# Attention and feed-forward layer on one core: the filler placed behind the values, small sums of the group normalisation on ScalarE, and three planned DMA times

## The chip, the cores and the metric

The kernel runs on one core of a Trainium2 chip. The metric is the device time of one execution in microseconds, the median of several runs. Engines are named as the profile names them: PE is TensorE's matmul, PEld its weight load, DVE is VectorE, ACT is ScalarE, POOL is GpSimd, SP is SyncE.

## The reference

The input x has the shape (4, 1024, 512). The layer is a differential attention, a group normalisation, an output projection, a residual and a layer normalisation, and behind them a feed-forward network with ternary weights, a residual and a layer normalisation.

```
q, k, v = x @ Wq, x @ Wk, x @ Wv          # 16 heads, 4 key/value heads, rotary positions
s1, s2  = q1 @ k1.T * scale + causal, q2 @ k2.T * scale + causal
diff    = softmax(s1) - lam * softmax(s2)
out     = diff @ v                        # (B, H, T, 64)
mean, var over (T, 64) of each head       # the group normalisation
out     = ((out - mean) * rsqrt(var + 1e-5) * gn_w + gn_b) * (1 - LAMBDA_INIT)
x       = layernorm(x + out @ Wo)
x       = layernorm(x + (silu(x @ up) * (x @ gate)) @ down)   # ternary weights
```

## The kernel before, in words

**Attention.** The work is 512 units of one query tile (128 rows) of one head, in both maps. Each goes through a chain over the engines: `scores` on PE (L1077, q against k, up to 1024 keys, one or two matmuls a map), `minimum` on DVE (L1421, mask, negative maximum, PSUM to SBUF), `exponent` on ACT (L1215), `factor` on POOL (L1346, L1347), `combine` on DVE (L1492, the difference of the two maps), `turn` on PE (L1058 and L1062, transposes of 128x128 blocks), `evict` on ACT (L1205, PSUM to SBUF), `values` on PE (L1096, a product with v that writes 64 of the 128 PSUM rows at a time, 32 or 48 matmuls in a run), and `product` on DVE (L1513, divides by the sums of the exponentials and writes `ra`). Long and short tiles alternate, so that four units always make the same amount of work. There are 129 runs of `values`.

**Group normalisation.** After eight pairs of units (a chunk; there are 32) DVE takes the statistics of `ra` (`moments`, L1518 to L1520), PE averages the mean over 64 rows with a tiny matmul (`mean`, L1181), DVE computes `spread`, four operations on one column each (L1526 to L1529: mean minus averaged mean, a copy of the averaged mean out of PSUM, the square, plus the variance), PE averages that (`variance`, L1184), DVE adds epsilon (`deviation`, L1533), POOL makes the factors and applies them (`group`, L1389 to L1392; `settle`, L1395), and SP stores the chunk (`store a`). A chunk's first `product` waits for the store of the chunk two before it, whose half of `ra` it writes.

**Filler.** Between the steps of the attention chain PE runs `fill` pieces: the projections of all batches (L1120, L1127, float32 weights loaded by ACT's queue into two buffers, `load w`, and x into six homes, `load x`), and, as soon as a batch's attention is stored, the output projection (L1141), the transposes of x1 (L1145), the up and gate products (L1154) and the down product (L1163). A piece takes about 1.7 us. In the first batch there is only projection to fill with.

**Who orders it.** The order on every engine is fixed when the kernel is built, by a list scheduler in the file (`in_order`, L495). It has a table of costs (`takes`), a table of what comes before what (`after`), the times at which DMAs count as landed behind their issue (`LANDS`), and strings of steps for each engine (`STRINGS`); it steps through planned time and gives each engine one head at a time. On PE it takes, of the heads that could start within a small window behind the earliest, the one of the lowest rank: scores (rank 0, window 0.4 us), mean, variance and totals (1), turn (2, 0.25 us), values (3), filler last and only if it is the earliest (4, 0.0). From unit 128 on scores are held to 3.75 us a unit. PSUM has eight banks; scores may hold four. The planned times set only the order: on the chip the engines wait for semaphores, and the instruction streams of each engine run strictly in the planned order.

The choice on PE, L616 and L617:

```
soon = min(h[0] for h in heads)
return min((h for h in heads if h[0] <= soon + FIRST[h[2].what][1]), key=lambda h: (FIRST[h[2].what][0], h[0]))
```

Of the kernel before, what the change touches and what calls it, by code (L numbers as in the profile page):

```python
# [10 lines left out]
ACT = mybir.ActivationFunctionType  # L11
ALU = mybir.AluOpType
# [24 lines left out]
CHUNKS = NH // 16  # L37
# [102 lines left out]
OF_KIND = {_kind: [j for j in PROJECTION + MIXING if j.kind == _kind] for _kind in PIECES}  # L140
# [59 lines left out]
def y_last(b):  # L200
# [6 lines left out]
TERN_AT = [100 + int(3 * i) for i in range(PREP)]  # L207

HAND_OVER = {"pe": .3, "act": .4, "dve": .3, "pool": .3}
LANDS = {"load q": 4.5, "load k": 7.5, "load v": 6.0, "store v": 7.0, "store rotated": 6.0, "store a": 4.5, "load a": 6.5,  # L210
         "store out": 2.5, "load wo": 9.0, "load x1": 8.0, "load weight": 12.0, "load x": 6.5, "load w": 6.5, "load rope": 5.0, "load lambda": 6.0, "load first": 2.5}


def width(n):
# [16 lines left out]
def takes(item):  # L231

    what, a, b = item
    if what == "scores":
        return 0.00042 * width(a) + (0.04 if width(a) > BANK else 0.03)
    if what == "turn":
        return 0.109 * blocks_of(a, b)[0] + 0.02
    if what == "values":
        return sum(0.22 * (STEPS[heads_of(duo)[0]].t + 1) for duo in duos_of(a)) + 0.24
    if what == "fill":  # L240
        return COST[a.kind] + 0.02
    if what == "exponent":
        return 0.27 + 0.00084 * width(a)
    if what == "evict":
        blocks, keys = blocks_of(a, b)
        if in_line(STEPS[a].duo) or blocks == keys:
            return 0.06 + 0.107 * blocks
        return 0.22 + (0.06 + 0.107 * keys if keys else 0)
    if what == "minimum":
        return 0.08 + 0.00104 * width(a)  # L250
    if what == "combine":
        return 0.13 + 0.00104 * width(a)
    if what == "empty":
        return {"E": 1.25, "O": 1.25, "wo": 1.5, "x1T": 0.61, "up": 0.61, "gate": 0.61,
                "y": 1.55 if a.i else 0.67}[a.kind]
    if what == "factor":
        return 1.4 if STEPS[a].r else 1.15
    return {"mean": 0.2, "variance": 0.2, "totals": 0.2, "copy": 0.55, "hidden": 0.55, "sum": 1.1,
            "lambda": 0.3, "normalise": 0.65, "high": 0.63, "early": 3.1, "product": 0.22, "moments": 1.55,
            "spread": 0.5, "deviation": 0.16, "ternary": 1.25, "all sums": 0.3, "scales": 0.3, "constants": 0.7, "minus lambda": 0.2,  # L260
            "load q": 1.0, "load k": 1.9, "load first": 0.5, "load x1": 0.5, "load wo": 0.48, "load a": 0.5, "store v": 0.45,
            "store rotated": 0.45, "store a": 0.45, "store out": 0.5, "load weight": 0.5, "load v": 0.5, "load lambda": 0.8, "lambda sums": 0.5,
            "hidden low": 1.32, "rsqrt": 1.5, "rotate": 1.35, "low": 1.3, "group": 1.5, "settle": 1.25, "side": 1.1}.get(what, 0.06)


def after(item):

    what, a, b = item
    out = []
# [96 lines left out]
        if a % 8 == 0 and a >= 16:  # L366
            out.append(ITEM("store a", a // 8 - 2))
    elif what == "moments":
        out = [ITEM("product", 8 * a + 7)]
    elif what == "spread":  # L370
        out = [ITEM("mean", a)] + [ITEM("settle", a - 1)] * (a > 0)
    elif what == "deviation":
# [65 lines left out]
def stored(b, h, u):  # L438
# [10 lines left out]
           [ITEM(what, c) for c in range(CHUNKS) for what in ("mean", "variance")], [ITEM("totals")]],  # L449
    "act": [[ITEM("exponent", n, m) for n, m in _maps], [ITEM("evict", n, h) for n, h in _halves],  # L450
            [ITEM("load rope", h) for h in range(2)], [ITEM("load lambda")], [ITEM("lambda")],
            *[[ITEM("copy", j) for j in OF_KIND[kind]] for kind in ("V", "x1T", "up")],
            [ITEM("hidden", j) for j in OF_KIND["gate"]], [ITEM("normalise", j) for j in LN_JOBS], [ITEM("sum", i) for i in range(PREP)],
            [ITEM("side", i) for i in range(PREP)],
            [ITEM("load x", p, c) for p in range(ONCE, len(PASSES)) for c in range(DC)], [ITEM("load w", i) for i in range(len(WLOADS))]],
# [2 lines left out]
            *[[ITEM("empty", j) for j in PROJECTION + MIXING if j.kind in kinds]  # L458
              for kinds in ("EO", ("x1T",), ("up", "gate"), ("wo", "y"))],
            [ITEM("early", j) for j in O_JOBS[:ROT_FIRST]], [ITEM("high", j) for j in O_JOBS[ROT_FIRST:]],  # L460
            [ITEM(what, c) for c in range(CHUNKS) for what in ("moments", "spread", "deviation")],
            [ITEM("lambda sums"), ITEM("minus lambda")], [ITEM("all sums"), ITEM("scales"), ITEM("constants")],
            [ITEM("ternary", i) for i in range(PREP)]],
    "pool": [[ITEM("factor", n) for n in _heads], [ITEM("hidden low", j) for j in OF_KIND["gate"]],
# [30 lines left out]
def in_order():  # L495
# [89 lines left out]
    def choose(e):  # L585
        now = free[e]
        heads = []
        for s, string in enumerate(STRINGS[e]):
            if at[e][s] < len(string):
                item = string[at[e][s]]  # L590
                r = ready(item, e)
                if r is None:
                    continue
                if item.what == "scores" and item.a and item.b == 0:
                    if item.a >= 128:
                        r = max(r, end[ITEM("scores", item.a - 16)] + PACE * 16)
                if item.what in LONG and factors:
                    other = ITEM("combine", factors - 1)
                    if other not in end:
                        continue  # L600
                    r = max(r, end[other])
                if banks_of(item):
                    found = banks(banks_of(item))
                    if found is None or item.what == "turn" and stuck(item) and sum(map(stuck, turned)) >= STUCK:
                        continue
                    if item.what == "scores" and in_scores + len(found) > SCORE_BANKS:
                        continue
                    r = max([r] + [bank_free[m] for m in found])
                heads.append((max(r, now), r, item, s))
        if e == "pe":  # L610
            filling = next_fill(now)
            if filling:
                heads.append((max(filling[0], now), filling[0], filling[1], None))
            if not heads:
                return None
            soon = min(h[0] for h in heads)  # L616
            return min((h for h in heads if h[0] <= soon + FIRST[h[2].what][1]), key=lambda h: (FIRST[h[2].what][0], h[0]))  # L617
        if not heads:
            return None
        soon = min(h[0] for h in heads)  # L620
        return min((h for h in heads if h[0] <= soon + 0.02), key=lambda h: h[1] - AHEAD.get(h[2].what, 0.0))
# [55 lines left out]
def layer_kernel(nc, x, x_cols, w_proj, wo, lams_in, gn, w_up, w_gate, w_down, rope, out):  # L677
# [13 lines left out]
    with ctx:  # L691
# [3 lines left out]
        def sem(name):  # L695
            return ctx.enter_context(nc.semaphore(name))
# [140 lines left out]
        s_gmv = sem("s_gmv")  # L837
        s_gm = sem("s_gm")
        s_rv = sem("s_rv")
        s_gv = sem("s_gv")  # L840
        s_norm = sem("s_norm")

# [17 lines left out]
        def multiplied(eng, duo):  # L860

            if duo % 2 and duo < DUOS - 1:
                eng.wait_ge(s_short, duo // 2 + 1)
            else:
                read_out(eng, "values", run_of(duo))
# [324 lines left out]
        def _(act):  # L1190
# [36 lines left out]
            def load_w(i):  # L1227
                if i >= 2:
                    act.wait_ge(s_ffull, INDEX[W_LAST[i - 2]] + 1)
                act.dma_start(wr[:, i % 2, :, :], w_proj[UNITS.index(WLOADS[i][3])]).then_inc(s_win[i % 2], 16)  # L1230
# [23 lines left out]
            def hidden_high(job):  # L1254
                f = HID[job]
                freed(act, job)
                nc.scalar.activation(hid[:, 0, job.i % 8, :], th[:, f % NTH, :], ACT.Copy).then_inc(s_hhi, 1)  # L1257

            for what, a, b in ORDER["act"]:
                if what == "exponent":  # L1260
                    exponent(a, b)
# [13 lines left out]
                    load_x(a, b)  # L1275
                elif what == "load w":
                    load_w(a)
                elif what == "load rope":
                    half = slice(a * BANK, (a + 1) * BANK)
                    act.dma_start(cs[:, :, half], rope[:, :, half]).then_inc(s_cs[a], 16)  # L1280
# [117 lines left out]
        def _(dve):  # L1398
            chain = [0]

            def link(ins):

                chain[0] += 1
                ins.then_inc(s_link, 1)
                dve.wait_ge(s_link, chain[0])
# [80 lines left out]
            for what, a, b in ORDER["dve"]:  # L1486
# [28 lines left out]
                elif what == "moments":  # L1515
                    for duo in range(8 * a, 8 * a + 8):
                        multiplied(dve, duo)
                    nc.vector.bn_stats(gst[:, 0, :], ra[:, a % 2, 0:BANK])  # L1518
                    link(nc.vector.bn_stats(gst[:, 1, :], ra[:, a % 2, BANK:T]))
                    nc.vector.bn_aggr(gmv[:, :], gst[:, :, :].rearrange("p h s -> p (h s)")).then_inc(s_gmv, 1)  # L1520
                elif what == "spread":
                    dve.wait_ge(s_gm, a + 1)
                    if a:
                        dve.wait_ge(s_norm, a)
                    bank, _ = BANK_OF[ITEM("mean", a)]
                    link(nc.vector.tensor_tensor(gsm[:, 1:2], gmv[:, 0:1], F[bank][:, 0:1], ALU.subtract))  # L1526
                    nc.vector.tensor_copy(gsm[:, 0:1], F[bank][:, 0:1]).then_inc(s_ffree[bank], 1)
                    link(nc.vector.tensor_tensor(gsm[:, 1:2], gsm[:, 1:2], gsm[:, 1:2], ALU.mult))
                    nc.vector.tensor_tensor(gsm[:, 2:3], gsm[:, 1:2], gmv[:, 1:2], ALU.add).then_inc(s_rv, 1)  # L1529
                elif what == "deviation":  # L1530
                    dve.wait_ge(s_gv, a + 1)
                    bank, _ = BANK_OF[ITEM("variance", a)]
# [69 lines left out]
```

## Time and profile before

| | us |
|---|---|
| median of 3 runs | 2219.04 (2218.55 to 2219.58) |
| the profiled execution | 2216.09 |
| its span, first to last instruction | 2214.3 |
| PE busy | 2141.2 (97%) |
| DVE busy | 1702.5 (77%) |
| ACT busy | 1431.8 (65%) |
| POOL busy | 1187.0 (54%) |

The profile is of one execution. Its busy time on PE contains weight loads that could not be hidden and the pipeline's latency at the end of each group of matmuls, so 97% is not 97% of the peak. The attention chain runs from about 53 us to 1941 us; what remains behind it is filler alone. In a timeline's row, the start and the duration of a merged group of matmuls give its end; the distance from the end of one group to the end of the next is what the second costs.

### The profile page before, as it was taken

The numbers are of one execution on the slowest core, as the hardware profiler recorded it, in microseconds if no ns is written. First come the engines' busy times: TensorE is split into PE (matmuls) and PEld (weight loads), VectorE is DVE, ScalarE is ACT, GpSimd is POOL, SyncE is SP. The second block draws the span as 40 slices with busy tenths as digits, with TensorE's granted clock in tenths as the row PEclk, the third lists the DMA queues.
The fourth block names the chain that finished last, engine by engine and source line by source line (L and its number), as shares of the span: only waits on it lengthen the run. The fifth ranks groups of instructions, "written<-read, shape, count | busy, mean of one in ns | idle before, by whom it ended". The sixth has DMA issues, their size and how long they took to land.

```text
span 2214.3 us, 41402 instructions
## 1 busy us (share of the span) xinstructions
PE 2141.2 (97%) x13442; PEld 1380.0 (62%) x13442; DVE 1702.5 (77%) x3829; ACT 1431.8 (65%) x3322; POOL 1187.0 (54%) x1919
## 2 busy tenths in 40 slices
PE   8999999899999999999999999999999999999998
PEld 4666667566666666666766666666666666644443
DVE  4888887889889888888778888878888888733333
ACT  0667777677687777767667767767677777622232
POOL 0676666677665555555545555655554555431232
PEclk9999999999999999999999999999999999999999
DMA  7666665867761213223632323342432112021000
GB/s 263 198 213 186 200 189 186 262 187 213 219 176 61 70 49 106 82 69 114 186 92 70 93 63 89 99 129 65 142 96 77 53 49 84 24 71 53 1 20 20
DMA packets 257428, 255.49 MB, mean 115 GB/s; under 512 B 31296, under 2 KB 199360, under 8 KB 255168
## 3 DMA queue, kind: packets, MB, share of 16 engines
q1 hardware_dynamic: 246016, 220.26, 33.2%
q10 hardware_dynamic: 11200, 32.58, 4.6%
q8 instruction: 112, 1.84, 0.3%
q14 instruction: 100, 0.82, 0.1%
HBM read 181.48 MB, written 71.30 MB: 114 GB/s over the span
## 4 chain that ended last, share of the span: by engine, by line
PE 79%; DVE 8%; issue 4%; POOL 4%; ACT 3%; DMA 1%; ACTq 0%; DVEq 0%; SPq 0%; POOLq 0%
PE PS L1154 19%; PE PS L1077 10%; PE PS L1096 10%; PE PS L1141 10%; PE PS L1163 9%; PE PS L1058 9%; PE PS L1120 8%; DVE e_long L1421 2%; PE PS L1127 2%; POOL linv L1346 1%; DVE e_long L1492 1%; ACT dt_long L1205 1%; PE PS L1062 1%; ACT e_long L1215 1%; POOL coef L1347 1%
## 5 line engine op out<-in xcount | busy, mean ns | idle before, releaser
L1215 ACT ACTIVATE e_long<-e_long,nmax 128x768 f32<-128x768 f32 (+3 forms) x512 | 505.9, 989 | 207.2 <-DVE nmax L1421 201.2
L1346 POOL TENSOR_TENSOR linv<-lsum,powers 128x2 f32<-128x2 f32 x512 | 405.4, 792 | 420.4 <-ACT e_long L1215 336.5
L1421 DVE CUSTOM_DVE_ANT_0 e_long<-PS,mask_b 128x768 f32<-128x768 f32 (+3 forms) x512 | 517.3, 1020 | 73.6 <-PE PS L1077 56.1
L1077 PE MATMUL PS<-kstk,qstk 128*128 128x384 f32 (+5 forms) x1536 | 465.7, 410 | 23.3 <-DVE nmax L1421 10.9
L1077 PEld LDWEIGHTS PS<-kstk,qstk 128*128 128x128 f32 x1536 | 268.6, 190 | 157.3 <-issue 92.7
L1492 DVE SCALAR_TENSOR_TENSOR e_long<-e_long,coef 128x1024 f32<-128x1024 f32 (+3 forms) x256 | 276.9, 1082 | 67.0 <-POOL coef L1347 66.6
L1205 ACT ACTIVATE dt_long<-PS 128x512 f32<-128x512 f32 (+3 forms) x544 | 258.5, 514 | 103.9 <-PE PS L1058 99.3
L1215 ACT ACTIVATE e_short<-e_short,nmax 128x384 f32<-128x384 f32 (+3 forms) x512 | 283.8, 559 | 17.1 <-DVE nmax L1421 16.1
L1359 POOL TENSOR_TENSOR hid<-th,hid 128x512 f16<-128x512 f32 x128 | 148.0, 1159 | 255.4 <-ACT hid L1257 132.8
L1120 PE MATMUL PS<-xT,wr 128*128 128x512 f32 x560 | 267.7, 606 | 13.8 <-DMA wr<-in_w_proj 8.7
L1058 PE MATMUL PS<-ident,e_long 128*128 128x128 f32 x1664 | 239.7, 275 | 11.9 <-DVE e_long L1492 8.7
L1347 POOL TENSOR_SCALAR coef<-lsum,linv,neglam 128x1 f32<-128x1 f32 x512 | 218.3, 426 | 53.4
L1421 DVE CUSTOM_DVE_ANT_0 e_short<-PS,mask_b 128x384 f32<-128x384 f32 (+3 forms) x512 | 237.7, 486 | 10.7 <-PE PS L1062 4.6
L1163 PE MATMUL PS<-down_t,hid 128*128 128x512 fp8e4 x1024 | 234.8, 379 | 0.4 <-ACT dt_long L1205 0.3
L1058 PEld LDWEIGHTS PS<-ident,e_long 128*128 128x128 f32 x1664 | 196.6, 142 | 55.5 <-issue 17.6
L1205 ACT ACTIVATE dt_short<-PS 128x512 f32<-128x512 f32 (+3 forms) x256 | 121.2, 474 | 136.8 <-PE PS L1062 106.8
L1096 PE MATMUL PS<-dt_long,vkv 128*64 128x128 f32 x3328 | 206.2, 274 | 0.0
L1154 PE MATMUL PS<-x_hi,gate_t 128*128 128x512 f16 x512 | 194.3, 380 | 1.0 <-DVE nmax L1421 1.0
L1154 PE MATMUL PS<-x_hi,up_t 128*128 128x512 f16 x512 | 194.2, 379 | 0.3 <-ACT dt_long L1205 0.3
L1154 PE MATMUL PS<-x_lo,gate_t 128*128 128x512 f16 x512 | 194.0, 379 | 0.0
L1154 PE MATMUL PS<-x_lo,up_t 128*128 128x512 f16 x512 | 194.0, 379 | 0.0
L1096 PEld LDWEIGHTS PS<-dt_long,vkv 128*64 128x64 f32 x3328 | 188.9, 138 | 0.3 <-issue 0.3
(125 smaller groups left out, 3275.2 us busy)
## 6 DMA issues: line engine op xcount, KB each, us to landing
qstk<-dq SPq DMA_DIRECT2D x512, 128.0 KB, 2.9
dq<-hl SPq DMA_DIRECT2D x25, 1024.0 KB, 5.5
wr<-in_w_proj ACTq DMA_DIRECT2D x48, 512.0 KB, 4.5
kstk<-dk SPq DMA_DIRECT2D x64, 256.0 KB, 5.2
da<-ra SPq DMA_DIRECT2D x32, 512.0 KB, 3.3
at_sb<-da SPq DMA_DIRECT2D x32, 512.0 KB, 4.1
wt<-in_w_up SPq DMA_DIRECT2D x16, 512.0 KB, 5.7
wt<-in_w_gate SPq DMA_DIRECT2D x16, 512.0 KB, 6.1
```

The source lines that it names most:

```text
L1058: last = nc.tensor.transpose(F[bank][:, k * P:(k + 1) * P], e1_of(n)[:, col:col + P], ident[:, :])
L1077: last = nc.tensor.matmul(slot[:, h, :], qstk[:, duo % 4, 2 * r + m, :].bitcast(F32R), kstk[:, g % 2, m, h * w:(h + 1) * w].bitcast(F32R), ...
L1096: last = nc.tensor.matmul(bank[64 * r:64 * r + 64, at:at + P], vkv[:, duo // 16 % 2, kb, :], dt_of(n)[:, kb, :], start=kb == 0, stop=kb == t)
L1120: last = nc.tensor.matmul(bank[:, :], wr[:, job.i % 2, c, at:at + P], x_part(job, c), start=c == 0, stop=c == DC - 1)
L1154: last = nc.tensor.matmul(bank[:, :], w[:, c, job.i * P:(job.i + 1) * P], part[:, c, job.h * BANK:(job.h + 1) * BANK], start=c == 0 and pa ...
L1163: last = nc.tensor.matmul(bank[:, :], hid[:, part, e, job.j * P:(job.j + 1) * P], down_t[:, 8 * job.i + e, :], start=e == 0 and part == 0, ...
L1205: copied = nc.scalar.activation(dt_of(n)[:, 4 * half:4 * half + here, :].rearrange("p k q -> p (k q)"), F[bank][:, 0:here * P], ACT.Copy)
L1215: nc.scalar.activation(e, e, ACT.Exp, bias=nmax[:, u % 8:u % 8 + 1], scale=-1.0, accum_out=lsum[:, n % 4, m:m + 1]).then_inc(s_exp, 1)
L1346: link(nc.gpsimd.tensor_tensor(linv[:, a % 8, :], lsum[:, a % 4, :], mone, ALU.pow))
L1347: nc.gpsimd.tensor_scalar(coef[:, a % 2:a % 2 + 1], lsum[:, a % 4, 0:1], linv[:, a % 8, 1:2], neglam[:, :], ALU.mult, ALU.mult).then_inc(s ...
L1421: nc.vector.tensor_tensor_reduce(out, slot, mask, -1.0, -NEG, ALU.add, ALU.min, nmax[:, u % 8:u % 8 + 1]).then_inc(s_negmax, 1)
L1492: nc.vector.scalar_tensor_tensor(e1_of(a)[:, 0:w], e2_of(a)[:, 0:w], coef[:, a % 2:a % 2 + 1], e1_of(a)[:, 0:w], ALU.mult, ALU.add).then_i ...
```

## The change

Four edits in one. The planner counts three kinds of DMA as landed later: `store rotated` 8 instead of 6 us, `load x` and `load w` 8 instead of 6.5 us. On PE, when the last step given out was `values`, a `scores` head ranks behind every other head that lies in its window. `spread` moves from DVE to ACT as a string of its own, is written as four activations, and is planned with 0.9 instead of 0.5 us. And `moments` of a chunk waits until the `spread` of the chunk before has been done, because the two now run on different engines and share `gmv`. The number of x homes stays six.

```
-LANDS = {... "store rotated": 6.0, ... "load x": 6.5, "load w": 6.5, ...}
+LANDS = {... "store rotated": 8, ... "load x": 8, "load w": 8, ...}

-            "spread": 0.5,
+            "spread": 0.9,

     elif what == "moments":
-        out = [ITEM("product", 8 * a + 7)]
+        out = [ITEM("product", 8 * a + 7)] + [ITEM("spread", a - 1)] * (a > 0)

+            back = order[e][-1].what == "values" if order[e] else False
+            return min((h for h in heads if h[0] <= soon + FIRST[h[2].what][1]),
+                       key=lambda h: (back and h[2].what == "scores", FIRST[h[2].what][0], h[0]))

 # ScalarE's stream (link: the engine waits for the instruction's own semaphore)
+                elif what == "spread":
+                    act.wait_ge(s_gm, a + 1)
+                    if a:
+                        act.wait_ge(s_norm, a)
+                    bank, _ = BANK_OF[ITEM("mean", a)]
+                    link(nc.scalar.activation(gsm[:, 3:4], F[bank][:, 0:1], ACT.Copy, scale=-1.0))
+                    nc.scalar.activation(gsm[:, 0:1], F[bank][:, 0:1], ACT.Copy).then_inc(s_ffree[bank], 1)
+                    link(nc.scalar.activation(gsm[:, 1:2], gmv[:, 0:1], ACT.Square, bias=gsm[:, 3:4]))
+                    nc.scalar.activation(gsm[:, 2:3], gsm[:, 1:2], ACT.Identity, bias=gmv[:, 1:2]).then_inc(s_rv, 1)

 # VectorE's stream, moments
+                    if a:
+                        dve.wait_ge(s_rv, a)
 # VectorE's stream, spread: taken out
-                    link(nc.vector.tensor_tensor(gsm[:, 1:2], gmv[:, 0:1], F[bank][:, 0:1], ALU.subtract))
-                    nc.vector.tensor_copy(gsm[:, 0:1], F[bank][:, 0:1]).then_inc(s_ffree[bank], 1)
-                    link(nc.vector.tensor_tensor(gsm[:, 1:2], gsm[:, 1:2], gsm[:, 1:2], ALU.mult))
-                    nc.vector.tensor_tensor(gsm[:, 2:3], gsm[:, 1:2], gmv[:, 1:2], ALU.add).then_inc(s_rv, 1)
```

## Rows read from the trace of the kernel before

**Rows 1.** The page: span, and the chain that ended last by engine.

```profile
span 2214.3 us, 41402 instructions
...
PE 79%; DVE 8%; issue 4%; POOL 4%; ACT 3%; DMA 1%; ACTq 0%; DVEq 0%; SPq 0%; POOLq 0%
```

**Rows 2.** Windows by stage: busy of PE, PEld, DVE, ACT, POOL, PEclk, DMA, GB/s.

```profile
0.00:600.00 600.00, 556.54 (x3290) 376.88 (x3292) 492.62 (x1083) 388.12 (x922) 372.68 (x537) 0.98 0.69 211
600.00:1941.00 1341.00, 1320.44 (x9047) 882.67 (x9044) 1111.92 (x2590) 970.16 (x2294) 744.57 (x1277) 1.00 0.30 89
```

**Rows 3.** Waits of PE, 0 to 600 us: total us, times, longest.

```profile
PE PS L1077 <- ACT dt_long L1205: 10.1, 12, 2.8
...
PE PS L1077 <- DVE nmax L1421: 8.6, 19, 1.7
PE PS L1120 <- DVE ra L1513: 3.3, 1, 3.3
```

**Rows 4.** Waits of PE, 600 to 1941 us, the largest.

```profile
PE PS L1058 <- DVE e_long L1492: 6.7, 7, 2.3
```

**Rows 5.** Timeline of PE (start us, us): first and last scores right behind values.

```profile
88.38 0.56 PE L1077 MATMUL PS<-kstk,qstk 128*128 128x320 f32 x2
...
1912.29 0.56 PE L1077 MATMUL PS<-kstk,qstk 128*128 128x320 f32 x2
```

**Rows 6.** Timeline of PE: scores behind filler, scores behind values, turns behind scores.

```profile
916.56 0.38 PE L1154 MATMUL PS<-x_lo,gate_t 128*128 128x512 f16 x1
916.59 0.82 PE L1077 MATMUL PS<-kstk,qstk 128*128 128x512 f32 x2
...
923.04 1.48 PE L1096 MATMUL PS<-dt_long,vkv 128*64 128x128 f32 x24
924.45 0.73 PE L1077 MATMUL PS<-kstk,qstk 128*128 128x512 f32 x2
925.02 0.49 PE L1058 MATMUL PS<-ident,e_short 128*128 128x128 f32 x3
```

**Rows 7.** Timeline of PE: turns of three blocks behind values.

```profile
1383.73 0.39 PE L1096 MATMUL PS<-dt_long,vkv 128*64 128x128 f32 x4
1384.05 0.44 PE L1058 MATMUL PS<-ident,e_short 128*128 128x128 f32 x2
1384.32 0.27 PE L1062 MATMUL PS<-ident,wide 128*128 128x128 f32 x1
```

**Rows 8.** Groups by form, weight loads: xcount | busy us, mean ns of one | idle before.

```profile
L1077 PEld LDWEIGHTS PS<-kstk,qstk 128*128 128x128 f32 x1536 | 268.6, 190 | 157.3 <-issue 92.7 <-DVE nmax L1421 25.5 <-ACT dt_long L1205 6.7
...
L1058 PEld LDWEIGHTS PS<-ident,e_long 128*128 128x128 f32 x1664 | 196.6, 142 | 55.5 <-issue 17.6 <-DVE e_long L1492 14.8 <-DVE nmax L1421 4.5
...
L1163 PEld LDWEIGHTS PS<-down_t,hid 128*128 128x128 f16 x1024 | 97.8, 98 | 107.6 <-issue 3.0 <-POOL hid L1359 1.4 <-ACT dt_long L1205 0.5
```

**Rows 9.** Groups by form: one of the four small operations of spread on DVE.

```profile
L1527 DVE COPY gsm<-PS 128x1 f32<-128x1 f32 x32 | 5.1, 158 | 1.1
```

**Rows 10.** Groups by form: ACT, exponent of the narrowest tile.

```profile
L1215 ACT ACTIVATE e_short<-e_short,nmax 128x128 f32<-128x128 f32 x128 | 50.5, 399 | 4.1 <-DVE nmax L1421 4.1
```

**Rows 11.** Line 1295 on ACT: duration ns min/median/max, first and last start.

```profile
L1295 ACT ACT_TABLE_LOAD  x1: 1283/1283/1283, 5.2 to 5.2; - x1
L1295 ACT ACTIVATE th<-th x1: 203/203/203, 16.4 to 16.4; 128x2 f32<-128x2 f32 x1
```

**Rows 12.** DMA issues, 0 to 600 us: count, KB each, median us from issue to landing.

```profile
wr<-in_w_proj ACTq DMA_DIRECT2D x41, 512.0 KB, 4.5
...
dq<-hl SPq DMA_DIRECT2D x17, 1024.0 KB, 5.5
```

**Rows 13.** DMA issues, 408 to 421 us.

```profile
da<-ra SPq DMA_DIRECT2D x1, 512.0 KB, 9.3
```

**Rows 14.** Timeline of DVE around the longest wait.

```profile
419.73 0.29 DVE L1513 TENSOR_TENSOR ra<-PS,dt_long 128x128 f32<-128x128 f32 x1 [3.98 <-DMA da<-ra]
```

**Rows 15.** Window at the lower clock: length, busy PE, PEld, DVE, ACT, POOL, PEclk, DMA.

```profile
419.40:426.20 6.80, 6.12 (x10) 3.26 (x11) 6.10 (x13) 1.03 (x2) 1.52 (x2) 0.50 0.51 110
```

More of the change, by code:

```diff
@@ L209 @@
 HAND_OVER = {"pe": .3, "act": .4, "dve": .3, "pool": .3}
-LANDS = {"load q": 4.5, "load k": 7.5, "load v": 6.0, "store v": 7.0, "store rotated": 6.0, "store a": 4.5, "load a": 6.5,
-         "store out": 2.5, "load wo": 9.0, "load x1": 8.0, "load weight": 12.0, "load x": 6.5, "load w": 6.5, "load rope": 5.0, "load lambda": 6.0, "load first": 2.5}
+LANDS = {"load q": 4.5, "load k": 7.5, "load v": 6.0, "store v": 7.0, "store rotated": 8, "store a": 4.5, "load a": 6.5,
+         "store out": 2.5, "load wo": 9.0, "load x1": 8.0, "load weight": 12.0, "load x": 8, "load w": 8, "load rope": 5.0, "load lambda": 6.0, "load first": 2.5}
 def width(n):
@@ L259, in takes @@
             "lambda": 0.3, "normalise": 0.65, "high": 0.63, "early": 3.1, "product": 0.22, "moments": 1.55,
-            "spread": 0.5, "deviation": 0.16, "ternary": 1.25, "all sums": 0.3, "scales": 0.3, "constants": 0.7, "minus lambda": 0.2,
+            "spread": 0.9, "deviation": 0.16, "ternary": 1.25, "all sums": 0.3, "scales": 0.3, "constants": 0.7, "minus lambda": 0.2,
             "load q": 1.0, "load k": 1.9, "load first": 0.5, "load x1": 0.5, "load wo": 0.48, "load a": 0.5, "store v": 0.45,
@@ L451 @@
             [ITEM("load rope", h) for h in range(2)], [ITEM("load lambda")], [ITEM("lambda")],
-            *[[ITEM("copy", j) for j in OF_KIND[kind]] for kind in ("V", "x1T", "up")],
+            *[[ITEM("copy", j) for j in OF_KIND[kind]] for kind in ("V", "x1T", "up")], [ITEM("spread", c) for c in range(CHUNKS)],
             [ITEM("hidden", j) for j in OF_KIND["gate"]], [ITEM("normalise", j) for j in LN_JOBS], [ITEM("sum", i) for i in range(PREP)],
@@ L460 @@
             [ITEM("early", j) for j in O_JOBS[:ROT_FIRST]], [ITEM("high", j) for j in O_JOBS[ROT_FIRST:]],
-            [ITEM(what, c) for c in range(CHUNKS) for what in ("moments", "spread", "deviation")],
+            [ITEM(what, c) for c in range(CHUNKS) for what in ("moments", "deviation")],
             [ITEM("lambda sums"), ITEM("minus lambda")], [ITEM("all sums"), ITEM("scales"), ITEM("constants")],
@@ L616, in choose @@
             soon = min(h[0] for h in heads)
-            return min((h for h in heads if h[0] <= soon + FIRST[h[2].what][1]), key=lambda h: (FIRST[h[2].what][0], h[0]))
+            back = order[e][-1].what == "values" if order[e] else False
+            return min((h for h in heads if h[0] <= soon + FIRST[h[2].what][1]),
+                       key=lambda h: (back and h[2].what == "scores", FIRST[h[2].what][0], h[0]))
         if not heads:
@@ L839, in layer_kernel @@
         s_rv = sem("s_rv")
+        s_alink = sem("s_alink")
         s_gv = sem("s_gv")
@@ L1257, in hidden_high, with link @@
                 nc.scalar.activation(hid[:, 0, job.i % 8, :], th[:, f % NTH, :], ACT.Copy).then_inc(s_hhi, 1)
+            done = [0]
+            def link(ins):
+                done[0] += 1
+                ins.then_inc(s_alink, 1)
+                act.wait_ge(s_alink, done[0])
             for what, a, b in ORDER["act"]:
@@ L1520, in _ @@
                     nc.vector.bn_aggr(gmv[:, :], gst[:, :, :].rearrange("p h s -> p (h s)")).then_inc(s_gmv, 1)
[L1521 to L1525, printed above, removed]
-                    link(nc.vector.tensor_tensor(gsm[:, 1:2], gmv[:, 0:1], F[bank][:, 0:1], ALU.subtract))
-                    nc.vector.tensor_copy(gsm[:, 0:1], F[bank][:, 0:1]).then_inc(s_ffree[bank], 1)
-                    link(nc.vector.tensor_tensor(gsm[:, 1:2], gsm[:, 1:2], gsm[:, 1:2], ALU.mult))
-                    nc.vector.tensor_tensor(gsm[:, 2:3], gsm[:, 1:2], gmv[:, 1:2], ALU.add).then_inc(s_rv, 1)
                 elif what == "deviation":
```

## The prediction

> **What bounds the kernel now.** I read the page first, then windows by stage, the waits of PE, and its timeline group by group. PE carries 79% of the chain that ended last, and no other engine more than 8% [rows 1]: a microsecond counts if PE's work gets shorter or an idle gap of PE closes. The windows part the run in two [rows 2]. From 600 to 1941 us PE is busy for 1320.44 of 1341 us, so only 20.6 us of idle time are there to be won. From 0 to 600 us it is busy for 556.54, idle for 43.5, of which 8.65 is the start. In that stage PE waits for ACT's evictions (10.1 us at scores) nearly as much as for DVE's minima (8.6) [rows 3]; later DVE's combine is the largest (6.7) [rows 4]. Behind 1941 us there is only filler, in an order that the change doesn't touch.
>
> The busy time itself holds a part that the order decides, seen in the timeline from end to end. Scores of two 512-column matmuls behind filler: 916.94 to 917.41, 0.47 us. The same behind values: 924.52 to 925.18, 0.66 us [rows 6]. The 0.19 us more is one weight load of scores (190 ns) [rows 8], hidden elsewhere and bare behind values. Three blocks of turns behind scores cost 0.33 us (925.18 to 925.51) [rows 6], behind values 0.47 (1384.12 to 1384.59) [rows 7]: 0.14 more, again its own weight load (142 ns) [rows 8]. So the run of values hides nobody's first weights, and who follows it pays for his: 0.19 for scores, 0.14 for turns, 0.19 for a projection or output-projection piece by the same float32 kind of load, 0.10 for an up, gate or down piece (98 ns) [rows 8].
>
> **The change part by part.** *No scores behind values.* Of 129 runs of values, I count 76 with scores right behind, the first and last at 88.38 and 1912.29 us [rows 5], and 51 with turns. The exits cost 76 x 0.19 = 14.4 us now. They don't vanish: another takes the place. In 71 of the 76 places turns come right behind the one to four scores, so in most the turn was nearly ready; I take 50 of 76 going to turns (0.05 us won each, 2.5 us) and 26 to filler. The next filler behind the 76 is 35 times of the float32 kind (nothing won), 39 times up, gate or down (0.09 won), two times the transposes of x1: half of 26 x 0.09 is 1.2 us. Sum 3.7 us won. Bounds: nothing (all float32 pieces) and 76 x 0.09 = 6.8 us. The scores are late by a group of turns or by one piece of 1.7 us, and what waits for them is DVE's minimum; from 600 us on the pace rule has them early enough, and ahead of that see the rival below.
>
> The Trainium skill has a rule that speaks against this part: in TensorEngine Tiling (Array Packing), Key Properties, a change of tiling mode drains the engine, and values are tiles of 64 columns between full ones. By that the exit is paid whatever follows, and were it one fixed price the part would win nothing. The trace agrees that everyone pays and shows prices that differ by follower (0.19 against 0.14 us).
>
> *Spread to ACT.* DVE loses four operations of 0.158 us [rows 9], 0.63 us a chunk, 32 x 0.63 = 20 us of its 1702. ACT gets four. The trace has no one-column activation out of PSUM; from below it is bounded by the 128x2 activation of 203 ns [rows 11], from above by the narrowest exponent, 399 ns for 128 columns with a bias read per row [rows 10]. Four make 0.81 to 1.6 us; I take 1.0, nearer the row without columns, with two waits of ACT for itself: 32 us on top of 1432. Behind it in ACT's stream stand exponents and evictions, and for the evictions PE waits. Were PE's waits proportional to the load of who ends them, DVE's 1.2% less would give back some 0.3 us of its 20 to 30, ACT's 2.2% more would take 0.4 of its 15: nothing. Uncovered in the first 600 us, where PE is exposed, ten chunks could give 6 us (DVE) or cost 10 us (ACT). Value: 0. One sentence on a page: ScalarE: Activation LUTs, What ACT_TABLE_LOAD costs, gives 186 ns plus 93 ns for a bias per row, by which the four would be some 0.93 us, an estimate; no run here shows it yet.
>
> *moments waits for the spread before.* That was done a chunk (about 60 us) earlier: nothing. The chain of a chunk gets some 0.5 us longer, and its store is needed only when the second chunk behind begins.
>
> *Loads counted as later.* Nothing on the chip takes another time; only the plan changes. In the first 600 us `load w` lands in a median 4.5 us and the store of rotated parts in 5.5 [rows 12], well inside even the old 6.5 and 6. PE's only wait for a load there is the start. So as a correction it wins little. But it redraws the order of the first 600 us, and with it the accidental gaps. The largest of them: a chunk's store took 9.3 us in a crowded stretch [rows 13], DVE's product stood 3.98 us for it [rows 14], PE 3.3 us [rows 3], and the clock granted there was 0.50 for 6.8 us, the 1.2 GHz level [rows 15]. A redrawn order probably breaks this one meeting (5 us with the slower matmuls behind it) and may make others. Bounds: 10 us won (some third of the 34.9 us idle behind the start) to 12 us lost. I take 1.3 us won, a quarter of that one gap.
>
> **The sum.** On the profiled execution, 2216.09 us = span 2214.3 + 1.8 around it: 3.7 + 0 + 1.3 = 5.0 us less, 2211.1. That execution is 2.95 us below the median of the runs shown, 2219.04, so the median to forecast is 2214.0.
>
> **Rivals.** *A, the late scores open the early gaps: slower.* Place: ahead of unit 128 (I count it at some 500 us in the timeline), where there is no pace and the only filler is projection. 19 of the 76 places lie before 600 us. If filler slips ahead there, minimum, exponent, factor, combine and turn all come up to 1.7 us later. For it: PE's longest idle gaps are already there, and scores are what it waits on [rows 3]; planned loads that land later thin out the filler as well. Against it: DVE is busy 82% of that stage [rows 2], so it has other things to do meanwhile. Half of 19 x 1.7 us reaching PE is 16 us, less the 5.0 won: 2219.04 + 11 = 2230; with a third of them 2225. It decides once more than 5 us, three such delays, reach PE in full.
> *B, the exits change hands and nothing else does: no difference.* Mostly float32 pieces take the places, 1 to 2 us are won (or none, were an exit one fixed price of 0.19 us whoever follows), the gaps elsewhere balance: 2217 to 2219. For it: the proportional balance of DVE and ACT is zero, and less than a percent of PE's time is touched.
> *C, the gaps close too: clearly faster.* The gap at 420 us goes (5 us), DVE's relief of 6 us shows in the early stage, with 4 us from the exits: 2204. Against it: some gap takes each gap's place in an order nobody tuned for chip times.
> *D, a reload of ACT's tables.* Square is new in the stream. The trace has one table load, of 1283 ns [rows 11]; were Square not in the set of the exponential, each chunk would load twice: 32 x 2 x 1.28 = 82 us on ACT, whose idle share is 35%; with a quarter reaching PE 2219 + 20 - 5 = 2234. The copies, identities, signs and absolute values of the kernel cost no second load, which speaks against it.
>
> **How the numbers follow.** About 0.2%, 4.4 us, is what a measurement of this kernel can tell from no change. The forecast's own case (2210 to 2217) has 0.40, C 0.17, B 0.18, A 0.23, D 0.02. The forecast's case lies with two thirds below 2214.6 (0.27) and one above. Faster: 0.27 + 0.17, and something of B, 0.46. Slower: A, D and a little of the forecast's case gone wrong, 0.26. Same: 0.28. The range reaches to C's 2204 and, for A, to 2227.
>
> **What would show it.** Exits: in the timeline of PE, nearly no scores right behind values; turns and filler there instead, at 0.14, 0.19 and 0.10 us. Spread: four activations a chunk on ACT that sum to 0.8 to 1.6 us, one table load in all. Gaps: PE's idle time from 0 to 600 us stays within 5 us of 43.5. Wrong would be: over 10 of the 76 places still with scores (the others not being ready within the window), an idle time of PE before 600 us over 50 us (A), or under 35 (C), or a stage from 600 to 1941 us whose idle time leaves 15 to 26 us.

## The result, and the profile after

The changed kernel takes 2237.34 us (2236.47 to 2238.66), the kernel before beside it 2219.31 us: a ratio of 1.0078 (95% interval 1.0062 to 1.0094), 18 us slower where 5 us faster was forecast, and outside the range of 2204 to 2227. Its profiled execution took 2236.47 us. All medians and ratios here are of executions in the same, undisturbed state: a single one, of the later kernel no_lands, ran at a granted clock of 0.496 throughout, took 4389.57 us and is left out.

Windows by stage of the changed kernel, with the columns of [rows 2]:

```profile
0.00:600.00 600.00, 551.00 (x3280) 375.44 (x3282) 485.83 (x1044) 394.56 (x955) 374.89 (x535) 0.98 0.67 208
600.00:1941.00 1341.00, 1310.81 (x8935) 873.80 (x8931) 1103.08 (x2491) 985.73 (x2381) 755.45 (x1277) 0.99 0.31 91
```

PE idles 49.0 us in the first stage (43.5 before) and 30.2 us in the second (20.6). Both worsened, and the second more. The granted clock over the whole span is 0.989, against 0.992 before, so part of the loss is slower matmuls and not idle time.

The exits, in the timeline of PE after:

```profile
904.91 1.70 PE L1100 MATMUL PS<-dt_long,vkv 128*64 128x128 f32 x28
906.54 0.44 PE L1062 MATMUL PS<-ident,e_short 128*128 128x128 f32 x2
906.82 0.27 PE L1066 MATMUL PS<-ident,wide 128*128 128x128 f32 x1
906.84 0.60 PE L1081 MATMUL PS<-kstk,qstk 128*128 128x384 f32 x2
```

Values end at 906.61, the three blocks of turns at 907.09: 0.48 us, against 0.47 in [rows 7]. No scores stand right behind values any more: of the 129 runs 126 are followed by turns, two by projections, one by a down piece.

Spread on ACT (columns: count | busy us, mean ns | idle before), and the table load:

```profile
L1298 ACT ACTIVATE gsm<-gsm,gmv 128x1 f32<-128x1 f32 x32 | 9.4, 294 | 1.0
...
L1297 ACT ACTIVATE gsm<-gmv,gsm 128x1 f32<-128x1 f32 x32 | 9.1, 286 | 0.0
...
L1296 ACT ACTIVATE gsm<-PS 128x1 f32<-128x1 f32 x32 | 5.5, 171 | 1.0
L1295 ACT ACTIVATE gsm<-PS 128x1 f32<-128x1 f32 x32 | 5.3, 167 | 16.3 <-PE PS L1185 16.3
...
L1316 ACT ACT_TABLE_LOAD x1 | 1.3, 1283 | 5.2 <-issue 5.2
```

The four sum to 0.92 us a chunk, and the only table load is still the first. The prices that the Trainium skill gives (ScalarE: Activation LUTs, What ACT_TABLE_LOAD costs) make 0.93 us for the four, an estimate; these rows agree. New is that ACT stood idle for 16.3 us in all until the averaged mean was there.

Three waits of PE that are new or grew (us in total, how often, the longest). The first is of values for evictions on ACT and was 5.5 us before. The second is the largest new gap; SP's queue and DVE around it follow:

```profile
PE PS L1100 <- ACT dt_long L1209: 9.0, 8, 2.8
...
PE PS L1131 <- DVE ra L1534: 6.2, 1, 6.2
...
PE PS L1131 <- issue: 3.9, 1, 3.9
```
```profile
1064.19 5.66 SPq L990 DMA_DIRECT2D wo_sb<-in_wo  x8
1069.89 0.43 SPq L965 DMA_DIRECT2D da<-ra  x1
```
```profile
1080.90 0.29 DVE L1534 TENSOR_TENSOR ra<-PS,dt_long 128x128 f32<-128x128 f32 x1 [6.55 <-DMA da<-ra]
```

POOL had the chunk ready (`settle`) at 1064.9 us; its store was issued at 1069.89, behind the eight loads of the next output weights, and landed 10.9 us later among them. DVE's product waited 6.55 us for it and PE 6.2.

**Where the time is.** For every group of matmuls in the timeline I took the distance from the end of the group before it, and as its floor the tenth percentile of that distance among groups of its kind, count and width. So these figures are estimates. What is above the floor is the exit of values (0.10 to 0.20 us each) or a gap; a gap includes what slower matmuls at the lower clock cost. Unit 128 is the end of the first batch.

| us | floor | exits | gaps to unit 128 | gaps to unit 512 | gaps behind |
|---|---|---|---|---|---|
| before | 2045 | 23.1 | 59 | 58 | 3 |
| changed | 2045 | 19.4 | 63 | 77 | 6 |

The exits gave back 3.7 us, as forecast. The gaps took 26 us. The rows add up to 2188 and 2210 us; 26 and 24 us of the two spans are in none of the columns, so it is the differences between the rows that count.

### The profile page after: what moved, and what is told of

Same layout as the page of the kernel before. It is cut to its first block and busy times, and to the rows that moved or that the text cites. A ratio compares the mean times of both kernels' runs of the same rounds, so it can differ in the third digit from the quotient of the medians.

```text
span 2234.5 us, 41401 instructions
## 1 busy us (share of the span) xinstructions
PE 2145.4 (96%) x13442; PEld 1380.2 (62%) x13442; DVE 1692.7 (76%) x3701; ACT 1455.9 (65%) x3450; POOL 1202.3 (54%) x1919
## 5 line engine op out<-in xcount | busy, mean ns | idle before, releaser
L1367 POOL TENSOR_TENSOR linv<-lsum,powers 128x2 f32<-128x2 f32 x512 | 414.3, 809 | 392.9 <-ACT e_long L1219 308.2
L1513 DVE SCALAR_TENSOR_TENSOR e_long<-e_long,coef 128x1024 f32<-128x1024 f32 (+3 forms) x256 | 276.7, 1081 | 74.1 <-POOL coef L1368 73.3
L1219 ACT ACTIVATE e_short<-e_short,nmax 128x384 f32<-128x384 f32 (+3 forms) x512 | 283.4, 558 | 17.1 <-DVE nmax L1442 16.3
L1368 POOL TENSOR_SCALAR coef<-lsum,linv,neglam 128x1 f32<-128x1 f32 x512 | 225.6, 441 | 53.4
```

What stands on the lines that cost most here:

```text
L1219: nc.scalar.activation(e, e, ACT.Exp, bias=nmax[:, u % 8:u % 8 + 1], scale=-1.0, accum_out=lsum[:, n % 4, m:m + 1]).then_inc(s_exp, 1)
L1367: link(nc.gpsimd.tensor_tensor(linv[:, a % 8, :], lsum[:, a % 4, :], mone, ALU.pow))
L1368: nc.gpsimd.tensor_scalar(coef[:, a % 2:a % 2 + 1], lsum[:, a % 4, 0:1], linv[:, a % 8, 1:2], neglam[:, :], ALU.mult, ALU.mult).then_inc(s ...
L1513: nc.vector.scalar_tensor_tensor(e1_of(a)[:, 0:w], e2_of(a)[:, 0:w], coef[:, a % 2:a % 2 + 1], e1_of(a)[:, 0:w], ALU.mult, ALU.add).then_i ...
```

## The experiments

Each kernel was measured beside the kernel before. Differences are of medians; ratios have their 95% interval. Four theories stand against each other at first. A: late scores open gaps (the rival of the prediction). L: the later planned DMA times do it. S: the activations on ACT do it. R, which the prediction had only as a term of 1.3 us: any edit of the planner redraws the whole order, and where the gaps then fall is a draw.

### One part at a time, and an edit that means nothing

`rule_only`: only the new choice on PE. `lands_only`: only

```
-"store rotated": 6.0 ... "load x": 6.5, "load w": 6.5
+"store rotated": 8 ... "load x": 8, "load w": 8
```

`act_only`: only spread on ACT, with its string, its cost and the wait of moments. `null_minimum`:

```
     if what == "minimum":
-        return 0.08 + 0.00104 * width(a)
+        return 0.081 + 0.00104 * width(a)
```

> The kernel before with the changed choice on PE alone (scores behind values rank last). Theory R (the order is redrawn and its accidental gaps move, whoever redraws it): exits cost 3.7 us less, gaps move by some 10 us in either direction, 2206 to 2226. Theory A (late scores open the early gaps of PE): 2227 to 2237, and PE's idle time before 600 us grows by 10 us. Theory L (the later planned loads do it): 2213 to 2217. Theory S (the four activations do it): 2213 to 2217.

> The kernel before with the three planned DMA times alone (8 us). Theory R: 2209 to 2231, no sign foreseen. Theory A: 2217 to 2221. Theory L: 2230 to 2240, with the loss before 600 us, where the projections are the filler. Theory S: 2217 to 2221.

> The kernel before with spread on ACT alone (four activations, planned 0.9 us, moments behind the spread before). Theory R: 2209 to 2231, no sign foreseen. Theories A and L: 2217 to 2221. Theory S: 2230 to 2240, with waits of PE for ACT's evictions up by more than 10 us over the whole attention.

> The kernel before with one planned cost one nanosecond larger (minimum 0.081 instead of 0.08 us plus its width): it means nothing and computes the same, but the planner's order differs from the 58th step of PE on. Theory R: moves by 5 to 15 us in either direction. Theories A, L and S, which blame a part of the change for the whole loss: within 4 us of 2219.

| | median, us | against before | ratio |
|---|---|---|---|
| rule_only | 2225.77 | +5.5 | 1.0028 (1.0017 to 1.0040) |
| lands_only | 2269.71 | +49.5 | 1.0223 (1.0208 to 1.0238) |
| act_only | 2230.67 | +10.4 | 1.0049 (1.0034 to 1.0064) |
| null_minimum | 2242.38 | +22.1 | 1.0097 (1.0080 to 1.0114) |

One nanosecond of a planned cost, with the same instructions in another order, loses more than the whole change does. That is R, and no theory that blames one part foresaw it; but R's own size for it, 5 to 15 us, was too small as well. The parts sum to 65 us, the change has 18. A's price for the rule alone (2227 to 2237) was too high. The DMA times alone lose more than twice the change, more than any theory had allowed (up to 2240). act_only lies inside both R's range and S's, but S's sign isn't there: PE's waits of scores and values for evictions are 12.1 us, against 16.1 before.

### Two more such edits

```
-"product": 0.22          (null_product)       -return 0.13 + 0.00104 * width(a)    (combine, null_combine)
+"product": 0.23                               +return 0.131 + 0.00104 * width(a)
```

> A second edit that means nothing: the planned cost of product 0.23 instead of 0.22 us, which redraws the order from PE's 113th step on. Theory R, sharpened: the order of before is a lucky one among its neighbours, and a redrawn one costs 5 to 25 us: 2224 to 2245. If the first such edit was the unlucky one instead: 2210 to 2222.

> A third edit without meaning: the planned cost of combine 0.131 instead of 0.13 us plus its width; the order differs from PE's 58th step on. Theory R, sharpened: 2225 to 2265, like the two others (22 and 42 us slower). If the order of before is an average one: 2205 to 2222.

`null_product` took 2261.31 us, 42.1 more (1.0188, 1.0174 to 1.0201); `null_combine` 2228.77, 9.1 more (1.0038, 1.0023 to 1.0053). The first lies above R's range (2224 to 2245), the second inside it (2225 to 2265). Three of three are slower, by 9, 22 and 42 us: the order of before is a lucky one among its neighbours. The windows of null_product show that both stages lose, as in the change, but here the first loses most:

```profile
0.00:600.00 600.00, 534.77 (x3117) 364.92 (x3118) 474.05 (x1041) 375.82 (x891) 353.19 (x514) 0.95 0.65 198
600.00:1941.00 1341.00, 1309.52 (x8945) 879.63 (x8945) 1115.61 (x2592) 971.45 (x2295) 761.11 (x1285) 1.00 0.32 95
```

PE idles 65 us in the first stage and is granted 0.95 of its clock there, against 43.5 us and 0.98 [rows 2]; in the second it idles 31.5 us, against 20.6.

### The other corners of the three edits

`no_lands` is the changed kernel with the old DMA times, `no_rule` the one with the old choice on PE, `no_act` the one with spread on DVE.

> The changed kernel with the three DMA times as before (rule on PE and spread on ACT, redrawn order). Theory R, sharpened (a redrawn order costs 5 to 50 us, whichever edit redraws it, and the parts don't add up): 2224 to 2245. If the parts add up (6 for the rule, 10 for spread): 2235 to 2237.

> The changed kernel without the rule on PE (DMA times and spread on ACT, redrawn order). If the parts add up (50 for the DMA times, 10 for spread): 2279 to 2281. Theory R, sharpened: anything from 2224 to 2270.

> The changed kernel without spread on ACT (rule on PE and DMA times, redrawn order), the last corner of the cube of three edits. If edits had prices of their own (6 and 50 us): 2275. Theory R, sharpened: anything from 2220 to 2270.

`no_lands` took 2217.39 us (-2.9; 0.9993, 0.9984 to 1.0003), `no_rule` 2226.96 (+6.6; 1.0032, 1.0018 to 1.0046), `no_act` 2245.09 (+25.4; 1.0116, 1.0099 to 1.0133). Neither of my figures for no_lands held: it is level with before, although two parts that lose 6 and 10 us alone are in it. no_rule and no_act lie inside the wide ranges of R, and far from the sums of their parts (2280 and 2275). The DMA times cost 49.5 us on the kernel before, 19.9 on top of the rule, 20.9 on top of both others, and give back 3.8 on top of spread. Their mean, 22 us, is the worst of the three, but four values from -4 to 50 are no price. One piece of it does come back: in all six kernels that were planned with them and in which SP's first steps are as planned, PE stands before its second group of V projections near 50 us, and in none of those planned without.

```profile
48.64 5.38 PE L1131 MATMUL PS<-wr,at_sb 128*128 128x256 f32 x16 [3.89 <-issue]
```

That is the changed kernel; the kernel before has 0.43 us of wait there.

### The edits without redrawing: the order pinned

Here the planner runs as before, and its finished lists are edited: `pinned_turns` puts turns ahead of the scores right behind values, where no bank and no earlier step on DVE forbids it (68 places).

```
+turns_first(ORDER):  values, scores.., turns..  ->  values, turns.., scores..      on PE only
```

`pinned_act` moves each spread from DVE's list to ACT's, at its planned time; `pinned_both` does both.

> The order of before kept on all engines and in all banks; only on PE, in 68 of the 76 places, the turns that follow the scores are put ahead of them, right behind the values. Theory R (the loss comes from redrawing the order): with no redrawing the exits cost 68 x 0.05 = 3.4 us less and the gaps stay within 2 us: 2214 to 2218. Theory A (late scores open PE's gaps): the scores are late here too, by 0.2 to 1.0 us in 68 places: 2224 or more.

> The order of before kept; only spread is taken out of DVE's stream and its four activations are put into ACT's stream at the same planned time. Theory R: the balance of DVE (20 us less) and ACT (25 to 30 us more) is near nothing: 2216 to 2223. Theory S (the activations themselves cost the time): 2228 to 2232, as where the order was redrawn with them.

> Both edits on the kept order, that is the changed kernel's two real changes without its redrawn plan. Theory R: the sum of the two, 2212 to 2220. Theories A and S: 2225 or more.

`pinned_turns` took 2230.98 us (+11.8; 1.0057, 1.0043 to 1.0071), `pinned_act` 2217.21 (-2.0; 0.9991, 0.9983 to 1.0000), `pinned_both` 2230.88 (1.0054, 1.0041 to 1.0066). So spread on ACT costs nothing that these runs can tell, which rules S out. But R's figure for the turns failed, and A's held: with nothing redrawn the exits cost 19.7 instead of 23.1 us, the 3.4 of the expectation, and the gaps 139 instead of 120. DVE's minimum waits for scores 56.1 us in the kernel before and 71.9 in pinned_turns. From 600 to 1941 us, in the kernel before, in pinned_turns and in the changed kernel, this wait (of the wide tiles, as above) is:

```profile
DVE e_long L1421 <- PE PS L1077: 42.8, 51, 2.9
```
```profile
DVE e_long L1445 <- PE PS L1101: 55.6, 61, 2.7
```
```profile
DVE e_long L1442 <- PE PS L1081: 40.7, 51, 2.4
```

In pinned_turns the scores do come late for DVE, and most of it lies where I had said that the pace rule covers it. That this wait is the way by which PE lost its time is argued, not shown: pinned_act has 65.1 us of it in all and lost nothing. In the changed kernel, where the planner made a new order around the late scores, the wait behind 600 us is no longer than before. So the pinned runs show what turns first would cost by itself, and not that the changed kernel pays it. PE's idle time of pinned_turns is 47.1 us to 600 us (+3.6) and 30.2 us from there to 1941 (+9.6), the latter from

```profile
600.00:1941.00 1341.00, 1310.84 (x8977) 872.17 (x8974) 1107.72 (x2580) 971.04 (x2289) 748.27 (x1277) 1.00 0.30 89
```

### Is it the lateness of scores, or any local shift?

A new theory, F, says that any local shift of this order costs time, whichever step becomes late.

`pinned_values` saves the same exits the other way round: the values go behind the scores, so that the scores come 1.9 us earlier (71 places). `pinned_best` adds spread on ACT.

```
+values_late(ORDER):  values, scores.., turns..  ->  scores.., values, turns..      on PE only
```

> The order of before kept on all engines and banks; on PE, in 71 places the run of values is put behind the scores that followed it, ahead of the turns. The exits cost 71 x 0.05 = 3.5 us less, as with turns first, but the scores come about 1.9 us earlier instead of later; the values come 0.3 to 1.4 us later. Theory A (late scores are what opens gaps): 2213 to 2217, faster than before. Theory F (any local shift of the tuned order costs, whichever step is late): 2222 to 2235.

> The same with spread on ACT at its old planned time. Theory A: 2211 to 2215, which would beat both kernels. Theory F: 2220 to 2233.

They took 2257.78 us (+37.5; 1.0173, 1.0156 to 1.0189) and 2256.82 (+36.5; 1.0170, 1.0155 to 1.0186). F had the sign, but at most 2235. Early scores with late values are worse than late scores. In the first 600 us the scores now wait for the minima that free their banks, with the values queued behind them: 22.8 us, which is 14.2 of PE's 14.5 us of new idle time there. The waits of PE in the first 600 us of pinned_values, scores for DVE's minima (8.6 us, 19 times, in [rows 3]):

```profile
PE PS L1096 <- DVE nmax L1440: 22.8, 27, 2.0
```

DVE's products waited 88.5 us for values, against 38.4 before. So F's sign stands, not A alone: the order of before loses by a shift either way, and moving either step by some microsecond costs more than the 0.05 us it saves.

### Closing the largest gap of the changed kernel

Two theories, on where the changed kernel's loss sits. G: in a few collisions that the new order made. D (not the prediction's rival of that letter): spread over many small gaps, and another opens where one is closed.

`after_store` moves the store of chunk 15 ahead of the eight weight loads; `after_both` also gives SP's first 32 steps the order of before; `after_three` also puts two loads of attention tiles ahead of two loads of x1.

```
-SP: load wo x8, store a 15                   -SP: load x1, load x1, load a 8, load q 143, load a 9
+SP: store a 15, load wo x8                   +SP: load a 8, load a 9, load x1, load x1, load q 143
```

> The changed kernel with nine steps of SP turned round in one place: the store of chunk 15 is issued ahead of the eight loads of the next output weights instead of behind them. Theory G (the loss sits in a few collisions that the redrawn order made): the gap of PE at 1081 us (6.2 us, and the lower clock behind it) closes: 6 to 9 us faster than the changed kernel, 2228 to 2232. Theory D (the loss is spread over hundreds of small gaps, and another one opens where one is closed): 2234 to 2238.

> The same, and SP's first 32 steps in the order that the kernel before has (keys loaded ahead of a store of rotated parts, the first queries ahead of a weight load). The gap of PE at 48 us (3.9 us) should close too. Theory G: 3 to 5 us less than with the store alone, 2223 to 2228. Theory D: 2232 to 2238.

> The kernel with two repairs of SP's order, and a third in the same crowded place: the loads of attention tiles 8 and 9 are issued ahead of the two loads of x1 that wait for the stores of the output. With the first two repairs the gap of PE had only moved, from the product (6.2 us) to the output projection that waits for tile 8 (8.2 us). Theory G: this closes it, 6 to 9 us less than with two repairs, 2230 to 2234. Theory D: the queue's next load or the crowded DMA engines hold the same piece, 2236 to 2241.

| | median, us | ratio to before | gap of PE near 1080 us, from |
|---|---|---|---|
| changed | 2237.34 | 1.0078 (1.0062 to 1.0094) | 6.2, product, for the store |
| after_store | 2241.68 | 1.0099 (1.0083 to 1.0114) | 7.8, output projection, for its tile |
| after_both | 2239.88 | 1.0091 (1.0075 to 1.0106) | 8.2, the same |
| after_three | 2231.44 | 1.0059 (1.0046 to 1.0072) | 3.6, the same |

The first repair did what it was to do: the store was issued ahead of the weight loads and landed in 5.8 us. It won nothing. A few microseconds on, the output projection of batch 1 stood for a tile whose load was queued behind the loads of x1, and these waited for output stores that were themselves behind the weight loads. PE in after_both and in after_three:

```profile
1085.99 3.75 PE L1162 MATMUL PS<-wo_sb,at_sb 128*128 128x512 f32 x4 [8.16 <-DMA at_sb<-da]
```
```profile
1082.50 3.03 PE L1176 MATMUL PS<-wo_sb,at_sb 128*128 128x512 f32 x4 [3.64 <-DMA at_sb<-da]
```

Only the third repair, at the last link, gave time: 0.3% or 7 us less than after_both, of which 4.5 are the shorter wait itself. G's range held for the third repair alone. D's mechanism, another gap opening, showed in the first two, though both lie above D's range (up to 2238). Some 12 us over before remain, and outside the start PE has no single gap over 4 us that could hold them.

### Is the changed kernel's own time a draw?

`after_null` is the changed kernel with the nanosecond of null_minimum.

> The changed kernel with the planned cost of minimum one nanosecond larger, which means nothing; its order differs from the changed kernel's from PE's 280th step on. Theory R, sharpened: 2220 to 2265, some 10 us from the changed kernel in either direction. If the changed kernel's three edits are what costs: within 4 us of 2237.

2230.93 us (1.0054, 1.0033 to 1.0075), 6 us less than the changed kernel. The two intervals overlap (1.0062 to 1.0094 and 1.0033 to 1.0075), so this alone doesn't settle it; with the three other such edits it fits. The gap near 1081 us isn't in this order: PE's longest waits behind the start are 3.9 and 3.3 us, and it still is 12 us slower than before.

The eleven kernels whose order the planner redrew after some edit lie at -3, +6, +7, +9, +10, +12, +18, +22, +25, +42 and +50 us against before. The five of them with the later DMA times have a mean of 22 us (7 to 50), the six without 14 (-3 to 42). In their timelines the floor is 2045 to 2047 us everywhere, the exits are 19.2 to 19.4 us with the rule and 23.3 to 23.7 without, and the gaps are what differs:

| gaps, us | before | no_lands | no_rule | act_only | null_combine | rule_only | after_null | changed | null_minimum | no_act | null_product | lands_only |
|---|---|---|---|---|---|---|---|---|---|---|---|---|
| to unit 128 | 59 | 52 | 61 | 54 | 64 | 60 | 56 | 63 | 67 | 69 | 83 | 79 |
| to unit 512 | 58 | 71 | 61 | 75 | 66 | 73 | 79 | 77 | 76 | 79 | 80 | 94 |

No kernel beat the one before by more than its measurement can tell: pinned_act (-2.0) and no_lands (-2.6) are level or barely better.

## Why the prediction was wrong

- **The exits: right, the size partly by luck.** 3.7 us forecast, 3.7 us estimated from the traces (23.1 to 19.4). But nearly all places went to turns (126 of 129) and not two thirds; that this wins as much as the forecast's mix of turns and filler (76 x 0.05 = 3.8 us) is chance. That the price of an exit is the follower's own weight load agrees with the sizes for scores and turns; for an up, gate or down piece no run shows it.
- **Spread on ACT: right.** 1.0 us a chunk taken, 0.92 measured; balance 0 taken, -2.0 us measured on the pinned order (interval of its ratio 0.9983 to 1.0000). The bound of 203 ns from below was too high for the two activations out of PSUM (167 and 171 ns). Rival D, a second table, did not occur.
- **The scores are late: wrong on the pinned order.** That "from 600 us on the pace rule has them early enough" failed there: turns first made that order 11.8 us slower although the exits gave back 3.4, some 15 us lost, with nearly three quarters of PE's new idle time behind 600 us. I had looked at whether PE waits for scores and not at who waits for PE: the page had DVE's minimum waiting 56 us for scores. In the changed kernel itself that wait behind 600 us didn't grow (42.8 to 40.7 us), so this isn't shown to be what it lost by.
- **The redrawn order: this is the step that sank the forecast.** "I take 1.3 us won", within 10 won and 12 lost. In its place the changed kernel lost 26 us in gaps (whatever share of them the rule has), and edits without any meaning lost 9 to 42 us. I had sized the term by one gap of the old order and taken its sign from there, with nothing to say how orders near it fare. I had reasoned that nothing on the chip takes another time and that a redrawn order breaks the one bad meeting. It did break it (the 3.98 us of [rows 14] is gone), and made another with 6.55 us. The term had been written under the later DMA times: with these taken back (no_lands) the other two parts, redrawn, are level with before.
- **Rival A** had the sign and, at 2225 to 2230, was the nearest, but for another stage: 5.5 us of PE's new idle time lie before 600 us and 9.6 behind. Of my signs, PE's idle time in the second stage (30.2 us against "15 to 26") spoke. That of the first, 49.0 us, was just outside "within 5 us of 43.5" and just under the "over 50" of rival A.
- **What stays open.** How much of the 18 us is the rule's lateness and how much the draw can't be read from the changed kernel, as in redrawn orders the rule cost 5.5 and 11 us and gave back 13 and 24. Whether the later DMA times have a price of their own is not settled either: the means of 22 us with them and 14 without come from ranges that overlap nearly in full, and the wait of 4 us near 50 us is all that repeats.

## What to carry to other kernels

Where a planner writes the order, the price of an edit is that of the new order, and its spread has to be measured before the edit is judged: change one planned cost by a nanosecond, a few times. To learn what the edit itself does, pin the old order and edit the finished list. Here ten of eleven redrawn orders were slower than the one before, by 0.8% in the mean of the eleven, so an edit worth 0.2% of saved work started far behind. How the order of before was come by isn't on record; where one is kept because it measured well, the same has to be expected. And before a step is made late, look at who waits for it, not only at whether its own engine has other work.

## What the runs showed of the hardware that was not expected

- A store of 512 KB lands in a median of 3.3 us behind 600 us and took 10.9 us from issue in the company of eight 256 KB loads, a store of 1 MB and three loads on ACT's queue, while the DMA engines were busy for 0.92 of the time:

```profile
wo_sb<-in_wo SPq DMA_DIRECT2D x8, 256.0 KB, 6.5
...
da<-ra SPq DMA_DIRECT2D x1, 512.0 KB, 10.9
```

- A one-column activation out of PSUM takes 167 to 171 ns, one with a bias read per row 286 to 294 ns; the four one-column operations of DVE in the kernel before took 150 to 159 ns [rows 9].
